# Relative attention rebuilt on the layout of the plain attention: scores in fp32r in two halves of the array, one trip of the window tiles over DRAM in each direction, masks on GpSimd

## What is computed

```
def _rel_idx(seq_len):
    r = jnp.arange(seq_len)
    dist = r[None, :] - r[:, None]
    return jnp.clip(dist, -MRP, MRP) + MRP          # MRP = 64
rk = embK[idx]
rv = embV[idx]
logits = jnp.einsum('bhqd,bhkd->bhqk', q, k) + jnp.einsum('bhqd,qkd->bhqk', q, rk)
w = jax.nn.softmax(logits, axis=-1)
out = jnp.einsum('bhqk,bhkd->bhqd', w, v) + jnp.einsum('bhqk,qkd->bhqd', w, rv)
```

## Time and profile before

| what | us |
|---|---|
| median of 3 runs | 5242.15 (5234.87 to 5248.39) |
| profiled execution | 5233.5 |
| its span, first to last instruction | 5231.8 |
| relative attention, first to last `ra_` instruction | 268 to 2712 |
| of it the loop over 32 heads, mark to mark | 367.3 to 2686.7 |
| plain attention, mark to mark | 3057.6 to 4507.2 |

### The profile page before, as it was taken

One profiled execution on the slowest core, in us unless ns is written; L12 is line 12 of the kernel. 1 busy time (PEld: TensorE's weight loads), 2 busy tenths in 40 slices (PEclk: granted clock), 3 DMA queues, 4 the chain that ended last, 5 costly groups with the idle time before them and its releaser, 6 DMA issues. The chain is left out here.

```text
span 5231.8 us, 98982 instructions
## 1 busy us (share of the span) xinstructions
PE 4445.3 (85%) x28530; PEld 2286.6 (44%) x28530; DVE 3855.6 (74%) x7286; ACT 3161.2 (60%) x5012; POOL 372.2 (7%) x385
## 2 busy tenths in 40 slices
PE   3759888888888888888875589999999999669998
PEld 1414444444444444444433333333333333359997
DVE  3767777777777777777754688888888888657775
ACT  1316666666666666666641137877877787426665
POOL 0000000000000000000000000000000000052322
PEclk9859999999999999999987779999999999869999
DMA  4645555556555455555544452322233233376664
GB/s 130 214 133 132 143 142 124 132 125 146 142 116 139 125 143 142 126 128 128 141 124 156 158 93 38 45 42 41 38 47 47 39 46 47 71 212 176 177 173 124
DMA packets 806473, 607.67 MB, mean 116 GB/s; under 512 B 92995, under 2 KB 764291, under 8 KB 799091
## 3 DMA queue, kind: packets, MB, share of 16 engines
q1 hardware_dynamic: 741251, 523.58, 41.6%
q0 software_dynamic: 19824, 24.52, 2.9%
q10 hardware_dynamic: 44800, 52.44, 2.8%
HBM read 355.14 MB, written 248.41 MB: 115 GB/s over the span
## 5 line engine op out<-in xcount | busy, mean ns | idle before, releaser
L885 ACT ACTIVATE ra_p<-ra_psS 128x1024 f32<-128x1024 f32 x1292 | 1266.8, 1021 | 813.1 <-PE ra_psS L992 467.2
L1336 DVE TENSOR_REDUCE pa_pm<-pa_psA 128x2 f32<-128x1024 f32 x1068 | 1261.0, 1219 | 177.1 <-PE pa_psA L1427 176.6
L772 DVE TENSOR_REDUCE ra_pm<-ra_psA 128x1 f32<-128x384 f32 (+1 forms) x2128 | 1281.8, 615 | 138.3 <-PE ra_psA L944 134.0
L1401 ACT ACTIVATE pa_p<-pa_psS 128x512 f32<-128x512 f32 x2054 | 1071.5, 601 | 286.3 <-PE pa_psS L1450 264.2
L944 PE MATMUL ra_psA<-ra_zs,ra_qs 96*128 96x512 bf16 x2128 | 843.3, 399 | 162.1 <-DVE ra_pm L772 134.4
L1427 PE MATMUL pa_psA<-pa_zs,pa_qs 48*128 48x512 f32 x2136 | 836.7, 475 | 70.6 <-DVE pa_recb L1367 30.5
L1450 PE MATMUL pa_psS<-pa_qs,pa_zs 50*128 50x512 f32 x2056 | 822.5, 469 | 52.5 <-ACT pa_p L1401 35.4
L992 PE MATMUL ra_psS<-ra_qs,ra_zs 99*128 99x512 bf16 (+3 forms) x2176 | 580.7, 347 | 107.5 <-ACT ra_p L885 107.5
L1450 PEld LDWEIGHTS pa_psS<-pa_qs,pa_zs 50*128 50x128 f32 x2056 | 347.5, 187 | 597.3 <-ACT pa_p L1401 564.2
L770 DVE TENSOR_TENSOR ra_sw<-ra_psA,ra_delta 128x128 f32<-128x128 f32 x1064 | 304.3, 286 | 403.8 <-PE ra_psA L944 385.3
L1035 PE MATMUL ra_psO<-ra_p,ra_vs 128*32 128x512 f32 (+3 forms) x4352 | 563.2, 544 | 0.1
(11 more groups left out here) (251 smaller groups left out, 4207.7 us busy)
## 6 DMA issues: line engine op xcount, KB each, us to landing
skewed_tables<-ra_p SPq DMA_DIRECT2D x272, 256.0 KB, 3.2
ra_skp<-skewed_tables SPq DMA_DIRECT2D x256, 256.0 KB, 4.7
mo_w_raw<-ffn_W SPq DMA_DIRECT2D x58, 1024.0 KB, 5.5
ra_delta<-skewed_tables SPq DMA_DIRECT2D x204, 256.0 KB, 3.1
skewed_tables<-ra_sw SPq DMA_DIRECT2D x192, 256.0 KB, 5.2
pa_qs<-q_halves SPq DMA_DIRECT2D x210, 128.0 KB, 4.9
pa_zs<-k_halves SPq DMA_DIRECT2D x210, 128.0 KB, 5.8
skewed_tables<-zero SPq DMA_DIRECT2D x8, 2048.0 KB, 11.9
```

Of the source, the lines that this page charges most:

```text
L772: dve.reduce_max(pm[:, p % 2, i, k:k + 1], bank[:, lo:hi], AX.X).then_inc(s_amax.h, 1)
L885: act.activation(pr[:, pos % NP, :], psS[:, pos % 2, :], ACT.Exp if kind == "E" else ACT.Copy).then_inc(s_cp.h, 1)
L1336: dve.reduce_max(pm[:, par, 2 * a:2 * a + 2], psA[w][:, :, :], AX.X).then_inc(s_am.h, 1)
L1401: act.activation(pr[:, i % NPR, :], psS[:, slot(i), :], ACT.Exp).then_inc(s_ex.h, 1)
```

## The change

`attention_stage` goes, and `rel_attention` takes its place, on the plan of `plain_attention`: two fp32r parts over 48 rows in two halves of the array, `ORDER` with the same pairs, one bank of `psS` (three banks) to a fill, double banks for scores, maxima in two rows of fp32r (`split_m`), `gather_heads` in place of `finals`, denominators over DRAM (here for every two heads), output stored transposed, so `out_stage` needs no transposes. The window:

- A double bank of scores holds 128 window columns at one end. VectorE takes the maximum of the other 896 and, in one operation, adds the diagonal, keeps `sw` and takes the maximum (`reduce_turn`). Its diagonals are `dl` and `dr`, masked.
- The table is made in the score banks (`relative`, in steps 0, 1, 4 and 5), copied by VectorE (`keep_r`), written once and read skewed once (`write_r`, `read_r`). POOL splits it by masks into right and left (`part_r`).
- After the exponential POOL masks the left and right tile and adds them into `pc` (`join_p`), SP writes that skewed and reads it straight (`write_p`, `read_p`), and POOL folds its two halves (`fold_p`). The column that falls on the seam comes from row sums that VectorE takes (`sum_right`). Kind "F" transposes the folded tile, ScalarE copies it to `ptr`, and `gather_heads` multiplies it by `evc`.

`ln_proj_stage` writes two fp32r parts in every mode; the zero fill is 4 MB, not 16; `window_masks` is new.

```diff
-    ring = []
-    if rel:
-        ring += [("F", c, 0) for c in range(4)]
-    for c in range(4):
-        ring += [("E", c, j) for j in range(7 if rel else 8)]
-        if rel:
-            ring += [("W", c, 0)]
-            if c % 2:
-                ring += [("R", c - 1, 0), ("R", c, 0)]
...
+RING = []
+for _c in range(4):
+    RING += [("E", _c, _j) for _j in range(14)] + [("W", _c, 0), ("W", _c, 1)]
+for _c, _at in reversed(tuple(enumerate((32, 40, 48, 56)))):
+    RING.insert(_at, ("F", _c, 0))
+NR = len(RING)
+R_STEPS = (0, 1, 4, 5)
+WX_STEP, WX_PER = 12, 2
+SUM_TURNS = (8, 10, 12, 14)
...
+            with sp.Fori(0, HEADS // U) as it:
+                for p in range(U):
+                    t, n = U * it + p, 2 * it + p // 2
+                    load_stack(t + 1, p + 1, 64, s_qe, STEPS * t)
+                    write_r(t + 2, p, 0)
+                    write_p(t, p, 0)
+                    read_r(t + 2, p, 0)
+                    write_r(t + 2, p, 1)
+                    write_p(t, p, 1)
+                    read_p(t, p, 0)
+                    write_p(t, p, 2)
+                    read_p(t, p, 1)
+                    read_r(t + 2, p, 1)
+                    write_p(t, p, 3)
+                    if p % 2 == 0:
+                        gather_denominators(t, n)
+                    write_r(t + 2, p, 2)
+                    write_r(t + 2, p, 3)
+                    if p == 2:
+                        load_v(t + 2, 4 * (t + 2))
+                    read_r(t + 2, p, 2)
+                    read_p(t, p, 2)
+                    if p % 2 == 0:
+                        spread_reciprocals(n)
+                    read_p(t, p, 3)
+                    read_r(t + 2, p, 3)
+                    load_stack(t + 3, p + 1, 0, s_qa)
+                    send_m(t + 1, p + 1)
+                    if p % 2 == 0:
+                        store_o(t, n)
...
+            def join_p(t, p, c):
+
+                i, q, w, n = 4 * c, p % 2, c % 2, PS_CUM[4] * t + PS_CUM[c]
+                s_we.wait(pool, NT * t + i + 4)
+                s_pw[(c - 2) % 4].wait(pool, 16 * (t + (c >= 2)))
+                s_sr.wait(pool, 4 * t + c - 1)
...
+                    keep(pc[:, w, :, :], sw[:, q, i:i + 4, P:W], LEFT, s_ps, n + 1)
...
+                    keep(tmp[:, w, :, :], sw[:, q, i:i + 4, 0:P], RIGHT, s_ps, PS_CUM[4] * t + PS_CUM[c + 1])
+                pool.tensor_tensor(out=pc[:, w, :, :], in0=pc[:, w, :, :], in1=tmp[:, w, :, :], op=ALU.add
+                                   ).then_inc(s_pc.h, 1)
...
+                    lay_v(t + 1, p + 1, it + 1 + (p + 1) // U)
+                    for c in range(4):
+                        join_p(t, p, c)
+                    for c in range(2):
+                        part_r(t + 2, c)
+                    for c in range(4):
+                        fold_p(t, c)
+                    for c in range(2, 4):
+                        part_r(t + 2, c)
...
+                dve.reduce_max(pm[:, q, i, 2 * left:2 * left + 1], psA[w][:, lo:lo + 2 * G - P], AX.X
+                               ).then_inc(s_far.h, 1)
+                dve.tensor_tensor_reduce(out=sw[:, q, i, P * left:P * left + P], in0=psA[w][:, at:at + P],
+                                         in1=(dl if left else dr)[:, i, :], scale=1.0, scalar=-3.0e38,
+                                         op0=ALU.add, op1=ALU.max, accum_out=pm[:, q, i, 2 * left + 1:2 * left + 2]
+                                         ).then_inc(s_am.h, 1)
...
+            def sum_right(t, c):
+                s_ps.wait(dve, PS_CUM[4] * t + PS_CUM[c + 1])
+                dve.reduce_sum(sr[:, 4 * c:4 * c + 4], tmp[:, c % 2, :, :], AX.X).then_inc(s_sr.h, 1)
...
+                else:
+                    s_fa.wait(pe, 4 * t + c + 1)
+                    for i in range(4):
+                        last = pe.transpose(dst[:, i * P:(i + 1) * P], blk_p[:, c % 2, i, 0:P], ident[:, :])
```

1222 lines of the change are left out of this document (569 added, 653 removed).

## The result

The changed kernel takes 5037.8 us (median of 4 runs, 5013.4 to 5046.8) against 5238.5 us (5234.5 to 5248.4): a ratio of 0.9607, 95% interval 0.9569 to 0.9645. That is 3.9% faster, inside the range of the forecast and 195 us above its value of 4843 us: about half of the gain that was forecast came.

The account below looks back on a forecast made before the run. The prediction took TensorE to end last in the relative attention's loop, VectorE next. 5233.5 - 384 (loop) - 13 (projection) - 11 (output) + 10 (entry, exit) = 4835 profiled; with the median 9 us higher, 4843 us. Range 4720 to 5100 us.

Parts of the forecast that it names:

- part 2: VectorE in the loop: 49.2 us of work a head, with a turn of 1.28 us.
- Rival (d): VectorE's fused add-and-maximum costs its upper bound, 0.57 us: 69.8 us a head, 5140 us; chance 0.09.
- sign of 52 to 54 us of busy VectorE: In the new loop's profile, VectorE would be busy for 52 to 54 us of each head.
- part 4: POOL and the window's trip: 38 us a head, 1.27 us per mask product of 128x512, first fold at 28.3 us.
- rival (e): POOL's masks become the bound and the kernel gets slower, 5400 us; chance 0.10 with another queue like it.
- The base of a head: Relative loop: VectorE's 49.2 us, plus 7.7 from the plain stage and 1.0 for bank hand-overs, 57.9 us a head.
- rival (b): Switching the array's tiling drains TensorE: 24 more switches, 4.1 us a head, 4940 us; chance 0.10.
- the price of the first fold: In the loop, TensorE stands 3.4 us for POOL's first fold; with VectorE's filled banks, 2.1 us a head was charged.
- the 7.7 us from the plain stage: Plain head's 45.3 us over its VectorE count of 37.6, for round trips and pass ends; added to each relative head.
- the forecast's 13 us: Projection ahead of the loop: a shorter wait for `rel_h` saves 1.6 us in each of 8 groups.
- Entry and exit: At the loop's two ends, uncovered table trips cost about 16 us, shorter clears give some back: +10 us.
- (c): Rival: DMA trips land later or SP's queue holds reads longer, 5.5 us more a head, 66, 5020 us; chance 0.10.

Follow-up runs that it names:

- first run: On POOL, folds 0 and 1 put ahead of the first two splits of the next table, against the changed kernel: 4867.4 us, ratio 0.9287 to the kernel before.
- third run: 36 idle transposes on TensorE before its wait for the first fold, added to the changed kernel: 5044.7 us, ratio 0.9634 to the kernel before.

## Why the forecast was right and where it was not

**VectorE (part 2) was right.** The fused operation is 280 ns with a second instruction of 83 ns, and in the timeline a maximum starts at 1110.12, its fused operation at 1111.12, the second instruction and the next maximum both at 1111.33: a turn is 1.21 us, where the count had 1.28. The maximum over 896 columns is 1088 ns, pitch 1.00. VectorE is busy 49.0 us a head, against 49.2 in the count. Rival (d) is refuted. The forecast's sign of 52 to 54 us of busy VectorE did not come; it went against its own count. The Trainium skill (VectorE: DVE Perf Modes, Two Vector instructions with no wait between them) has an accumulating operation as two instructions, and the trace agrees with 280 and 83 ns; it moved nothing.

**POOL's products (part 4) were right.** 1.27 to 1.28 us for 512 columns, the fold 1.265, so the broadcast mask costs nothing extra. POOL is busy 1131.9 / 32 = 35.4 us a head, and rival (e) is refuted. From the gate to the end of the first fold it took 32.1 - 16.3 = 15.8 us, in the forecast 15.65.

**The base of a head was right within 1.2 us.** 57.9 us without stalls, of which 1.6 belong to the ends of passes (the plain stage has 45.3 a head and 43.7 inside a pass), so 56.3 inside one. The run with the folds first has 57.6 in its undisturbed heads, and with the sums earlier on top they take 57.1. TensorE has less room than the forecast thought: in one of the 57.6 us, all at full clock, it is busy for 53.4, 93%, as in the plain stage (94%), where the forecast counted 47.3. Part of this is the way of counting, since the plain head is 38.6 in the forecast's pitches and 42.5 busy. Whether TensorE or VectorE with its hand-overs sets these 57 us no run took apart. A set of four transposes keeps it for 0.59 us at full clock (four in 0.44 in the earlier trace rows). These rows are of the changed kernel's timeline:

```profile
1273.26 0.66 PE L1402 MATMUL ra_psS<-ident,ra_blk 128*128 128x128 f32 x4
1273.85 0.50 PE L1351 MATMUL ra_psA<-ra_zs,ra_qs 48*128 48x512 f32 x1
...
1274.85 1.06 PE L1422 MATMUL ra_psO<-ra_p,ra_vs 128*32 128x512 f32 x8
1275.85 0.50 PE L1391 MATMUL ra_psS<-ra_qs,ra_zs 50*128 50x512 f32 x1
```

0.15 us a set more, and 1.00 for a weighing as before (0.99). That is at most 12 x 0.15 = 1.8 us a head for rival (b), not its 4.1. The Trainium skill (TensorEngine Tiling (Array Packing), Key Properties) says that a changed tiling mode drains TensorE; the 0.15 us may be that, but no run here took it apart from the transposes' own time, and between pairs and weighing no gap shows.

**The step that failed: the price of the first fold.** The forecast had the fold at 28.3 us from the head's start (29.8 in POOL's count, which the rest of this paragraph uses), TensorE wanting it 3.4 us earlier, and charged 2.1 us, plus 0.5 for later folds. Measured inside a pass: 65.0 us with the wait and 57.5 without, 7.5 us. Three things were missed. First, the gate: VectorE ends `sum_right` 0 at 16.0 us, not at 14.2, because it waits for banks four times for over 0.2 us in the head's first turns (1.11, 0.34, 0.23 and 1.24 us, the last for the gathered head), waits which I had spread over the whole head. With 0.5 us on the joins the fold ends 2.3 us later, and TensorE takes it up at 26.5 where it comes early enough (first run): 5.6 us of delay, not 3.4. (The forecast's place for it, 26.4 in this count, was right.) Second, the discount: by the sum below the banks that VectorE had in hand absorbed none of it. Third, the half clock, which the forecast did not have: 10.2 or 13.7 us at half clock around the wait, 3.9 us of them behind it, which cost 1.7 us (third run: 31.1 us instead of 32.8). 5.6 + 1.7 makes 7.3 of the 7.5.

**The ends of passes were mis-sized.** Inside the 7.7 us from the plain stage they cost 1.6 us a head. Here the mean, 68.15, lies 3.15 above a head inside a pass: the hole of 2.95 us and the half clock behind it come in the part of the head in which POOL's gate lies, and the first head takes 84 us. Together: (65.0 - 58.9) + (3.15 - 1.6) = 7.65 us, which is 68.15 - 60.5, and 32 x 7.65 = 245 us.

**Around the loop it went better.** The stages ahead gained 33 us, the forecast said 13. TensorE's rows in the groups of the projection (76 to 262 us before, 76 to 228 after):

```profile
L409 PE MATMUL rel_psU<-rel_hT,w_qkv_t 128*128 128x512 f32 x192 | 101.7, 694 | 16.5 <-ACT rel_hT L350 16.5
...
L401 PE MATMUL rel_psT<-ident,rel_h 128*128 128x128 f32 x64 | 12.5, 360 | 27.5 <-DVE rel_h L253 27.5
```

```profile
L381 PE MATMUL rel_psU<-rel_hT,w_qkv_t 128*128 128x512 f32 x192 | 88.2, 618 | 15.3 <-ACT rel_hT L329 15.3
...
L373 PE MATMUL rel_psT<-ident,rel_h 128*128 128x128 f32 x64 | 9.6, 298 | 13.7 <-DVE rel_h L246 13.6
```

The wait for `rel_h`, on which the forecast's 13 us rested, fell by 13.9 us: that term was right. What it put at nothing is TensorE's own work: the same matmuls were busy for 16.4 us less (141.81 to 125.45), at a granted clock of 0.99 in place of 0.87. That the shorter waits brought the clock up is the likely reason, but no run took the two apart. The output stage gave 12 us (11 forecast). Entry and exit, put at +10, gave 14.5 back, and the plain attention took 5. So -20 -1 -24.5 +5, with the loop's +245 about 205 us: the profiled span of 5040 against 4835.

**Rivals.** (c) has the loop's size nearly (66 us a head) for another reason: the read lands as counted (4.6 us after its issue, 4.7 in the count), the skewed write 1.1 us later (4.3, not 3.2), and neither sets the first fold, since POOL works almost without a break from the third join to it. "TensorE's wait is for POOL and not for the trip" was borne out as far as the row goes, and moved by moving POOL's queue.

## What to carry to other kernels

When a stage is bounded by one engine and another one feeds it through a queue, count the feed's chain to the microsecond against the place where it is wanted, from the end of the real wait that opens it and with the waits of the first turns there, not spread over the loop. A stall that is found so must not be discounted for buffers unless a row shows them, and it can cost more than its own length: here 5.6 us of lateness and the half clock behind them were 7.3 us of head. The cheap cure is the order on the idle engine's queue (one swap of two loops: 3.3%); reordering a shared DMA queue put off whatever stands behind the moved trip, first the maxima that TensorE needs (115 us of waits, 4.7% of the time) and then the denominators that VectorE needs, and each time the kernel was slower than without it. When such an edit backfires, look first at the waits of the engine that bounds the stage: the wait of POOL was the new one that was looked for, and TensorE's was the larger one.

## What the runs showed of the hardware that I had not expected

- TensorE's granted clock falls to its lower level (1.2 of 2.4 GHz) already ahead of the long wait, while the engine is still working. In the changed kernel (same columns as the windows above; the wait itself is the first row):

```profile
1262.60:1266.00 3.40, 0.00 (x0) 0.00 (x0) 1.30 (x3) 0.00 (x0) 3.09 (x5) 0.50 0.68 207
```

```profile
1225.00:1251.20 26.20, 23.74 (x195) 12.07 (x193) 21.44 (x47) 21.79 (x46) 12.91 (x13) 1.00 0.67 135
1251.20:1256.20 5.00, 4.30 (x28) 2.23 (x29) 5.00 (x10) 3.41 (x7) 4.52 (x5) 1.00 0.48 140
1256.20:1269.90 13.70, 10.26 (x40) 4.45 (x38) 6.57 (x14) 3.21 (x6) 10.34 (x12) 0.50 0.64 192
```

  TensorE was busy 86% and more of both stretches ahead of the fall, had short waits of 0.2 to 0.4 us among its pairs, and then ran at half clock for 6.4 us before it stood. Half clock made up 574 us of the changed kernel's loop and 309 us with the folds first.
- The hole of about 3 us behind a pass's end made a head 9.9 us longer here in most passes, and 4 to 8 us in the plain stage; in other runs, with 3.4 or 6.8 us of half clock behind the same hole instead of 17 or more, a head of the relative stage was only some 4 to 5 us longer than the shortest of its run.
- An operation with an accumulator reads it out in an instruction of its own of 83 ns, and the pair costs no more than an add of that size: the maximum behind it starts together with the read-out, 0.21 us after the fused operation.
- A small `v` load of 64 partitions took SP 2.30 us to issue (1.75 to 4.47 in nine times), in a queue where others take 0.35 to 0.5 us; the one behind it, of the same size, took 0.52. Why is not shown.
